# Hybrid attention and expert kernel: eight staging places for projected parts, and one maximum instruction per diagonal bank

## What is computed

```python
q = (x @ Wq).reshape(b, s, H, D).transpose(0, 2, 1, 3)      # H = 16 heads of D = 16
k = (x @ Wk).reshape(b, s, H, D).transpose(0, 2, 1, 3)
scores = jnp.einsum('bhqd,bhkd->bhqk', q, k)
scores = jnp.where(causal[None, None], scores, NEG) + bias   # bias in layer "a" only
w = jax.nn.softmax(scores / jnp.sqrt(jnp.float32(D)), axis=-1)
ctx = jnp.einsum('bhqk,bhkd->bqhd', w, v).reshape(b, s, e)
return ctx @ Wo + bo
```

## Time and profile before

| what | value |
|---|---|
| median of three runs | 2054.69 us |
| the profiled execution, its own time | 2051.69 us |
| its span in the profile | 2049.9 us |
| mean granted TensorE clock in the span | 0.858 of full speed |
| attention layer "a", core | about 60 to 545 us |
| attention layer "b", projections and core | about 1014 to 1560 us |
| expert layers | about 560 to 1012 us and 1580 us to the end |

### The profile page before, as it was taken

How to read it: one execution, slowest core, us unless ns; L and a number is a source line. 1 busy time by engine, 2 the same in 40 slices (tenths; PEclk the granted TensorE clock), 3 DMA queues, 4 the chain that set the end, 5 groups by cost and what they waited for, 6 DMA issues and landing times.

```text
span 2049.9 us, 36691 instructions
## 1 busy us (share of the span) xinstructions
PE 1679.9 (82%) x12464; PEld 1071.0 (52%) x12464; DVE 1475.6 (72%) x3241; ACT 1117.7 (55%) x1975; POOL 692.8 (34%) x778
## 2 busy tenths in 40 slices
PE   7899999999778799890197999999997787899910
PEld 6445454444556677770084444444454565777710
DVE  6678888886487855884555788888873877558843
ACT  2154747567366676660041347575674576677710
POOL 6000101001257375457730001010001575564466
PEclk9578979899889999995595679898998899899965
DMA  7350221300255576664234500505000755566643
GB/s 204 104 67 2 32 34 25 41 2 7 66 228 170 173 209 188 192 208 135 77 104 124 64 2 2 63 2 63 1 2 11 272 163 176 160 199 207 204 148 115
DMA packets 123276, 217.59 MB, mean 106 GB/s; under 512 B 16380, under 2 KB 92044, under 8 KB 118812
## 3 DMA queue, kind: packets, MB, share of 16 engines
q1 hardware_dynamic: 98520, 148.10, 26.5%
q0 software_dynamic: 24576, 67.14, 12.0%
HBM read 124.20 MB, written 90.46 MB: 105 GB/s over the span
## 4 chain that ended last, share of the span: by engine, by line
PE 57%; DVE 13%; DMA 11%; POOL 7%; issue 7%; ACT 3%; SPq 1%; DVEq 0%; ACTq 0%; POOLq 0%
PE late_banks L1584 14%; PE late_banks L1542 11%; PE exp_banks L1570 8%; PE late_banks L1402 6%; PE exp_banks L1419 6%; POOL ring_t L1008 5%; DMA ring_t<-token_rows,index_t 4%; DVE chunk_max_t L1990 3%; PE late_banks L1435 3%; DMA expert_rows<-outs_t 3%; DVE inter_t L1874 2%; PE late_banks L1548 2%; PE exp_banks L1435 2%; PE late_banks L1377 2%; POOL ring_t L1003 2%
## 5 line engine op out<-in xcount | busy, mean ns | idle before, releaser
L1229 ACT ACTIVATE probs_t<-exp_banks 128x1024 f32<-128x1024 f32 (+3 forms) x640 | 538.7, 895 | 348.6 <-PE exp_banks L1570 347.2
L1990 DVE TENSOR_REDUCE chunk_max_t<-late_banks 128x1 f32<-128x512 f32 (+1 forms) x960 | 602.4, 682 | 111.8 <-PE late_banks L1542 89.6
L1088 POOL TENSOR_SCALAR_AFFINE_SELECT probs_t<-probs_t 128x512 f32<-128x512 f32 x128 | 81.2, 635 | 861.2 <-ACT probs_t L1229 861.2
L1584 PE MATMUL late_banks<-probs_t,values_t 128*32 128x512 f32 (+3 forms) x2560 | 322.4, 580 | 9.9 <-POOL probs_t L1088 9.5
L1402 PE MATMUL late_banks<-tokensT_t,fetched_t 128*128 x2048 | 300.8, 292 | 10.8 <-issue 5.0
L1008 POOL DMA_INDIRECT ring_t<-expert_rows,rows_of_t x256 | 243.3, 950 | 180.8 <-DVE x_sb_t L1888 118.2
L1003 POOL DMA_INDIRECT ring_t<-token_rows,index_t x256 | 248.6, 971 | 146.6 <-PE late_banks L1377 88.3
L1874 DVE TENSOR_TENSOR inter_t<-late_banks,silu_t 64x256 f32<-64x256 f32 x512 | 217.4, 425 | 95.5 <-ACT silu_t L1174 84.6
L1402 PEld LDWEIGHTS late_banks<-tokensT_t,fetched_t 128*128 128x128 f32 x2048 | 256.8, 197 | 41.0 <-issue 21.6
L1542 PE MATMUL late_banks<-contextT_t,Qp_t 50*128 50x512 f32 (+7 forms) x640 | 249.9, 531 | 16.9 <-DVE part_lo_t L1931 8.9
L1419 PE MATMUL exp_banks<-fetched_t,inter_t 64*128 64x128 f32 x2048 | 188.7, 304 | 47.1 <-DVE inter_t L1874 45.2
(11 more groups left out here) (222 smaller groups left out, 1913.8 us busy)
## 6 DMA issues: line engine op xcount, KB each, us to landing
expert_rows<-outs_t SPq DMA_DIRECT2D x256, 256.0 KB
weights_t<-in_experts SPq DMA_DIRECT2D x8, 1728.0 KB, 13.1
Qp_t<-q_parts SPq DMA_DIRECT2D x36, 256.0 KB
weights_t<-in_experts SPq DMA_DIRECT2D x4, 2112.0 KB, 9.7
Kp_t<-k_parts SPq DMA_DIRECT2D x24, 256.0 KB
q_parts<-part_hi_t SPq DMA_DIRECT2D x16, 256.0 KB, 5.6
...
```

The lines of the kernel that those rows point to most:

```text
L1229: act.activation(probs[:, e % NP, 2 * p:2 * p + 2, off:QB], exp_banks[sq % 2][:, :, off:QB], ACT.Exp, scale=D ** -0.5).then_inc(exp_done, 1)
L1584: last = pe.matmul(pv_banks[n % NPV][32 * h:32 * h + 32, off:QB], values[:, j, GH * g + h, :], probs[:, e % NP, h, off:QB], start=(j == 0) ...
L1990: op = dve.tensor_reduce(chunk_max[:, slot, p, r, c], bank[:, 0:n].rearrange("q (p k) -> q p k", p=len(parts)), AX.X, ALU.max)
```

## The change

**Staging.** NSTAGE becomes 8. Places 0 to 3 stay, places 4 and 5 are new tiles at the end of the same area, places 6 and 7 are the first 2048 columns of `w_raw`, the unsplit weights. The last products of K0 and K1 of each half (n mod 8 of 6 and 7) use the latter and so wait for the semaphore `w_split`, that is, until GpSimd has split all weights of the layer. Q0 and K0 now wait for no store of their layer, Q1 waits for the stores of Q0, K1 for those of K0. SyncE's order stays. Its wait ahead of the first row maxima now names eight places: the stores of Q1 and K1.

**Maxima.** A bank with two diagonal rows holds row 0 first and then row 2. One reduction takes it as four pieces of 128 columns and writes four neighbouring maxima. `chunk_max` gets six columns for each row, preset once by GpSimd, and a copy for each of the four blocks b; the rows stand in the order 0, 2, 1, 3, so that the last column of row 0 and the first three of row 2 are neighbours. The final reduction to `neg_max` reads all 96 values of a query tile's 16 rows in every block, where it read 16 x (b + 1). The planner counts one instruction of 512 columns for every bank.

**A setting.** `dynamic_dma_scratch_size` is 8192: the region for descriptors of GpSimd's DMAs is half as large. That makes room for the new tiles.

```diff
-NSTAGE = 4
+NSTAGE, NSTAGE_HEAD, NSTAGE_TAIL = 8, 4, 2
 NMAX, NPV = 3, 1
+NCHUNK = 6
...
-    diagonal += [(hh, [(p, 2, b), (p, 0, b)]) for p in range(2) for hh in range(2)]
+    diagonal += [(hh, [(p, 0, b), (p, 2, b)]) for p in range(2) for hh in range(2)]
...
+def chunk_row(r):
+
+    return (0, 2, 1, 3)[r]
+
+
+def chunk_col(b, r, c):
+
+    return c + (2 if r == 0 else 3) if c < b else NCHUNK - 1 if r == 0 else 0
...
-            if parts[0][1:] == (1, b):
-                dve += 152 + QB / 0.96
-            else:
-                for _, r, c in parts:
-                    dve += 152 + part_width(b, r, c) / 0.96
+            dve += 152 + QB / 0.96
...
+        chunk_max = tile("chunk_max", [P, NB, GH, TPB, NCHUNK])
...
-        part_hi = [tile(f"part_hi{i}", [P, QB], F32R, pre) for i in range(NSTAGE)]
-        part_lo = [tile(f"part_lo{i}", [P, QB], F32R, pre) for i in range(NSTAGE)]
+        part_hi = [tile(f"part_hi{i}", [P, QB], F32R, pre) for i in range(NSTAGE_HEAD)]
+        part_lo = [tile(f"part_lo{i}", [P, QB], F32R, pre) for i in range(NSTAGE_HEAD)]
...
+        for i in range(NSTAGE_HEAD, NSTAGE_HEAD + NSTAGE_TAIL):
+            part_hi.append(tile(f"part_hi{i}", [P, QB], F32R, pre))
+            part_lo.append(tile(f"part_lo{i}", [P, QB], F32R, pre))
+        for i in range(NSTAGE - NSTAGE_HEAD - NSTAGE_TAIL):
+            part_hi.append(w_raw[:, 2 * i * QB:(2 * i + 1) * QB].bitcast(F32R))
+            part_lo.append(w_raw[:, (2 * i + 1) * QB:(2 * i + 2) * QB].bitcast(F32R))
...
-        chunk_max = tile("chunk_max", [P, 2, GH, TPB, NB], F32, core)
...
+            pool.memset(chunk_max[:, :, :, :, :], VLOW).then_inc(chunks_set, 1)
...
                         if n >= NSTAGE:
                             act.wait_ge(part_out[n % NSTAGE], 32 * (n // NSTAGE))
+                        if n % NSTAGE >= NSTAGE_HEAD + NSTAGE_TAIL:
+                            act.wait_ge(w_split, w_ready(phase[1], W_ORDER[phase[1]][-1]))
...
+                dve.wait_ge(chunks_set, 1)
...
-                            if bn >= 2:
-                                dve.wait_ge(neg_done, bn - 1)
+                            if bn >= NB:
+                                before = max(n for n in range(bn) if BLOCKS[n % len(BLOCKS)][1] == b)
+                                dve.wait_ge(neg_done, before + 1)
...
-                            op = dve.tensor_reduce(chunk_max[:, slot, p, r, c],
+                            op = dve.tensor_reduce(chunk_max[:, b, p, chunk_row(r), chunk_col(b, r, c)],
                                                    bank[:, 0:n].rearrange("q (p k) -> q p k", p=len(parts)), AX.X, ALU.max)
                         else:
-                            end = 0
-                            for p, r, c in parts:
-                                begin, end = end, end + part_width(b, r, c)
-                                op = dve.tensor_reduce(chunk_max[:, slot, 2 * p + hh, r, c:c + 1], bank[:, begin:end],
-                                                       AX.X, ALU.max)
+                            p = parts[0][0]
+                            first = chunk_row(0) * NCHUNK + chunk_col(b, 0, b)
+                            pieces = chunk_max[:, b, 2 * p + hh, :, :].rearrange("q r c -> q (r c)")[:, first:first + TPB]
+                            op = dve.tensor_reduce(pieces, bank.rearrange("q (i k) -> q i k", i=TPB), AX.X, ALU.max)
...
-                            dve.tensor_reduce(neg_max[:, slot, :, :], chunk_max[:, slot, :, :, 0:b + 1], AX.X, ALU.max,
-                                              negate=True).then_inc(neg_done, 1)
+                            rows = chunk_max[:, b, :, :, :].rearrange("q h (l u) c -> q h u l c", l=2)
+                            dve.tensor_reduce(neg_max[:, slot, :, :].rearrange("q h (u l) -> q h u l", l=2), rows,
+                                              AX.X, ALU.max, negate=True).then_inc(neg_done, 1)
...
-    nc = bacc.Bacc("TRN2", target_bir_lowering=False, num_devices=1)
+    nc = bacc.Bacc("TRN2", target_bir_lowering=False, num_devices=1, dynamic_dma_scratch_size=8192)
```

1 line of the change is left out of this document (added).

## The result

Twenty runs of each kernel gave 2033.9 us after the change (2024.9 to 2043.8) and 2046.2 us before it (2030.9 to 2061.7): ratio 0.9936, interval 0.9918 to 0.9955. The gain is 12 to 13 us where 4.8 were forecast. Of these 16 us, 8.5 are the starting point: the forecast set out from a median of three runs, 2054.69 us, and twenty runs give 2046.2. The other 7.5 us are gain that the forecast didn't have. The profiled execution spans 2034.2 us, 15.7 us less than the one before.

What follows compares the result with a forecast made beforehand. It took TensorE, 57% of the chain and hardly idle in the cores, as pacing; 0.5 + 2.4 - 0.5 + 2.4 = 4.8 us less gave 2046.9 us profiled, median 2050 us; 8-in-10 range 2035 to 2065 us.

Steps and rivals of the forecast that it cites:

- Part one, eight places: Start of each attention core: products begin up to 12.0 us earlier together, but a full DMA queue leaves 0.5 us gained.
- The two waits in series: Core start: two waits for the DMA queue, Q1's stores then K1's stores, of which the change removes only the first.
- The rival that the start moves whole: Core start: K1's stores land earlier with their issue, all 12.0 us kept in place of 0.5; 2038 us, chance 0.12.
- Part two, one reduction: VectorE's diagonal banks: 0.11 us saved each, 14.1 us in all, 2.4 on the path; wider final reduction costs 0.5 us.
- The order: Ends of b = 3 blocks in groups 1 and 2: maxima four banks further ahead, 2.4 us gained, bounds 0 and 9.6.
- The clock with the good sign: Cores: a tenth less of the 282 us at 1.2 GHz, time 14 us shorter; 2036 us, chance 0.07.
- the bad sign: Cores: a tenth more time at 1.2 GHz, the clock returning later in b = 3 blocks; 2064 us, chance 0.07.
- VectorE as the pacer of the whole core: Cores: TensorE's busy time hides waits for banks, so the whole 14.1 and 9.6 us come through; 2031 us, chance 0.08.
- The gathers: GpSimd's gathers: the halved descriptor region holds only two, about 150 gathers slow down, 19 us more; 2069 us, chance 0.03.
- The list: Signs to check: core starts, rows near 72 us, TensorE idle 5 us, reduction 684 ns, engines' busy times, clock, gathers.
- The sign that was set for the clock: Cores: a shift of the mean granted clock by more than 0.02 would show the forecast wrong.

Runs made afterwards that it cites:

- S: The eight staging places, put into the kernel before together with the smaller descriptor region and nothing else: ratio 0.9975 to before.
- C: The smaller descriptor region of 8192 bytes; put alone into the kernel before: ratio 0.9987 to before.
- sp: Kernel before with eight staging places, smaller descriptor region and the planner's new bank cost, still two reductions a bank: ratio 0.9928 to before.
- p_only: Kernel before with only the planner's new cost of a bank, so every engine has the new order: ratio 0.9929 to before.
- rows_first: Kernel after with SyncE's wait for the last Q1 and K1 stores moved behind the rows of blocks (0, 0) and (0, 1): ratio 0.9893 to before.
- r_only: Kernel before with only the one reduction and its wider final reduction, in the old order: ratio 1.0008 to before.
- rp: Kernel before with the one reduction and the planner's new order, still four staging places: ratio 0.9927 to before.
- d110: Kernel after with the planner counting 110 ns beside a bank's columns in place of 152; 11 banks alone ahead of (1, 3) and (2, 3): ratio 1.0010 to before.
- fill_g12: Kernel after with TensorE computing each bank of maxima that stands alone ahead of blocks (1, 3) and (2, 3) twice: ratio 0.9955 to before.
- c_only: Kernel before with the descriptor region of 8192 bytes and nothing else: ratio 0.9987 to before.
- g1_only: Kernel after with the order of before, except the new order from block (0, 3) to (1, 2), ahead of (1, 3): ratio 0.9994 to before.
- all_again: The changed kernel itself, unaltered, run once more on the chip of its parts: ratio 0.9941 to before.
- d64: Kernel after with the planner counting 64 ns beside a bank's columns in place of 152; 0 and 2 banks alone ahead of (1, 3) and (2, 3): ratio 0.9946 to before.
- c20: Kernel after with the planner taking TensorE at 2.0 columns a ns in place of 2.3; no banks alone ahead of (1, 3) and (2, 3): ratio 0.9951 to before.

## Why the prediction was wrong

**Part one, eight places: right.** The core's first product was forecast near 56.2 us and came at 56.00; the idle time left was forecast at 1.4 us and was 1.41. The rows were to go out near 72 us and went at 71.33. The first `qk` came 0.95 us earlier than before in layer "a" (74.70 and 75.65 us). S, measured alone with C, is 0.9975 with 1 in its interval, and sp equals p_only. The two waits in series, of which only the first goes, are shown by `rows_first`. The rival that the start moves whole (2038 us) gives nearly the measured time and is still wrong: its mechanism is not there.

**Part two, one reduction: mechanism right, size too large, worth nothing.** The four-piece reduction takes 685 ns for a forecast 684. VectorE's busy time on the page fell from 1475.6 to 1468.7 us, 6.9 us and not the 12 to 14 that were to be seen. With the 1.7 us that the wider final reductions add, the 128 banks save 8.6 us, 0.07 us each where the sum has 0.11. The 2.4 us on the path cannot be found: r_only is 1.0008, and rp equals p_only. The final reduction at 253 ns (forecast 247) is 0.2 us more in all.

**The order: this step failed.** It said that a moved bank costs about what it saves, took a quarter of 9.6 us, 2.4 us, and set the upper bound at 9.6. The order is worth 12.8 us in the four stretches that it touches most. By the division above, with twelve stretches of the new order, the terms are, for both layers:

- the stretch of maxima alone: 2.8 + 2.9 us shorter, 11.5 us in all, or 0.72 us a bank, where the step counted VectorE's 0.60;
- what the moved banks cost in the mix: 1.8 + 1.1 us, 5.8 us in all, 0.36 us a bank. So about half of what is saved is kept, 5.7 us, and not a quarter;
- the low clock behind the stretch: 14.9 us before and 7.4 us after for block (1, 3), no difference for (2, 3) (9.3 and 9.3 us). Half of 7.5 us in each layer is 7.5 us in all; by the measured 0.43 us for each us it is 6.4 us, and the mix then costs 4.8 us. The sum had no such term; it stood among the rivals.

The range failed with the same step. The three-run median that it set out from was 8.5 us high, which is chance; with 2046.2 us as its start it would have reached down to 2026.5 us.

**The rivals.** The clock with the good sign (2036 us, chance 0.07) is about half of what happened, 6.4 to 7.5 of 13.0 us, and its place, the end of the b = 3 blocks, is right: 268 to 292 us has 0.72 where the earlier trace rows has 0.57. `d110` looks like the bad sign: 17.5 us low behind the first `qk` of (1, 3), a second fall ahead of the end of (2, 3), and the whole gain given back. The sum should have had a term for the clock, since the row of 0.57 told that the stretch had a state to lose or win. The rule of the Trainium skill that the prediction cited ("TensorE: Matmul & The Clock Gate", section "A second HAM failure mode: psum-queue depth-cycling") lays the fall to short idle moments of TensorE. The later fall in `fill_g12`, 4.0 us ahead of the first `qk` where after has 6.9, agrees with it; no run here shows the idle moments themselves. VectorE as the pacer of the whole core fell with r_only, though VectorE does pace the stretches alone. The gathers fell with c_only: 0.9987, and a mean of 962 ns where `r_only` and `p_only`, on the same chip with the full region, have 958 and 961. The Trainium skill's count of descriptors ("DMA: Bandwidth & Descriptors", section "The descriptor swizzle") had this rival add nothing, and c_only agrees.

**The list.** Right: both core starts, rows near 72 us, TensorE idle for over 5 us behind its six banks, the reduction, the gathers. Missed: VectorE's busy time, and TensorE's, which was to stay nearly the same and fell from 1679.9 to 1665.3 us on the page, 14.6 us of the 15.7 that the span lost. The sign that was set for the clock did not fire: the cores have 0.86 and 0.84 for 0.84 twice (56 to 496 and 1076 to 1516 us), a shift of 0.02 at most. A mean over the core is too coarse to show a difference that sits in some 10 us of it.

**What stays open.** What decides how long the clock stays at 1.2 GHz once the mix is back. The same order gave 7.0 and 19.4 us in the two layers of `g1_only`; after and `all_again`, the same kernel, gave 6.8 and 11.4 us in layer "a"; the new order has 5.7 to 11.4 us in twelve stretches and the old one 9.7 to 19.7 us in ten. So the order seems to move the length but does not set it. That 0.42 to 0.5 us of each us is the cost rests on lengths that happened to differ from profile to profile; a run that changes the low time behind and nothing else was not found. Why `d64` and `c20` gain as much as after while `d110` gains nothing is known only as far as the single profiles go: `d64` takes 105.1 and 107.5 us for the first stretch and 91.5 and 97.1 us for the second. What brings the second fall in `d110` is open too.
